# Epilogue of a graph layer: where the table additions, the biases and the output bias are computed

## What is computed

```python
h = relu(layernorm(x))                                     # nodes, 6250 x 64
msg = relu(concat(h[dst], edge_attr) @ W1a + b1a) @ W1b + b1b
summed = segment_sum(msg, src); counts = segment_sum(1, src)
agg = summed / max(counts, 1)
out = x + relu(concat(h, agg) @ W2a + b2a) @ W2b + b2b
```

## Time and profile before

| what | us |
|---|---|
| median of three runs | 1584.05 |
| profiled execution | 1595.53 |
| its span | 1593.7 |
| TensorE busy | 1468.8 (92%) |
| VectorE busy | 1422.9 (89%) |
| Pool busy | 1215.1 (76%) |
| ScalarE busy | 1023.7 (64%) |

### The profile page before, as it was taken

One profiled execution on the slowest core, in us unless ns is written; L12 is line 12 of the kernel. 1 busy time (PEld: TensorE's weight loads), 2 busy tenths in 40 slices (PEclk: granted clock), 3 DMA queues, 4 the chain that ended last, 5 costly groups with the idle time before them and its releaser, 6 DMA issues. The chain is left out here.

```text
span 1593.7 us, 76970 instructions
## 1 busy us (share of the span) xinstructions
PE 1468.8 (92%) x31106; PEld 1401.0 (88%) x31106; DVE 1422.9 (89%) x4766; ACT 1023.7 (64%) x2192; POOL 1215.1 (76%) x804
## 2 busy tenths in 40 slices
PE   4378999999999989999999999999999999999937
PEld 3167999999999989999999999999999999999935
DVE  7977999999999979899999989999999999999937
ACT  5167666666666656667676766766766666666405
POOL 5347878778787778878787787788777788777864
PEclk8679999999999999999999999999999999999978
DMA  5657766776767666676676766766766677676643
GB/s 173 232 111 117 124 109 111 124 110 110 125 109 125 107 99 110 110 123 113 110 125 110 120 110 112 121 109 117 117 111 120 106 117 118 109 121 108 96 60 122
DMA packets 278693, 186.57 MB, mean 117 GB/s; under 512 B 190215, under 2 KB 274692, under 8 KB 277569
## 3 DMA queue, kind: packets, MB, share of 16 engines
q1 hardware_dynamic: 173358, 152.31, 38.8%
q0 software_dynamic: 104976, 29.30, 26.8%
HBM read 147.32 MB, written 34.17 MB: 114 GB/s over the span
## 5 line engine op out<-in xcount | busy, mean ns | idle before, releaser
L523 POOL DMA_INDIRECT sums<-vv,sidx x726 | 1158.5, 1596 | 328.8 <-issue 172.4
L1242 PE MATMUL l_ps<-area 128*128 128x64 bf16 (+1 forms) x21000 | 766.7, 193 | 7.7 <-issue 1.6
L1242 PEld LDWEIGHTS l_ps<-area 128*128 128x128 bf16 x21000 | 730.8, 98 | 28.7 <-issue 14.5
L698 ACT ACTIVATE area<-l_ps 64x392 bf16<-64x392 f32 x1400 | 684.5, 489 | 74.1 <-PE l_ps L1228 49.0
L949 DVE TENSOR_SCALAR area<-iota,local 128x640 bf16<-128x640 int16 x1400 | 482.8, 409 | 4.9
L1228 PE MATMUL l_ps<-r_d,oh 128*128 128x196 bf16 x4200 | 482.6, 249 | 2.8 <-ACT area L698 1.4
L1228 PEld LDWEIGHTS l_ps<-r_d,oh 128*128 128x128 bf16 x4200 | 345.2, 97 | 17.0 <-ACT area L698 3.2
L934 DVE TENSOR_SCALAR oh<-iota,rank 128x640 bf16<-128x640 int16 x846 | 285.1, 403 | 0.0
L681 ACT ACTIVATE r_d<-z_ps 128x384 f32<-128x384 f32 x423 | 207.6, 491 | 84.6 <-PE z_ps L1198 74.2
L686 ACT ACTIVATE vv<-c_ps 128x396 f32<-128x396 f32 x121 | 60.5, 500 | 265.3 <-PE c_ps L1217 179.3
L956 DVE TENSOR_TENSOR dense<-l_ps,dense 128x325 f32<-128x325 f32 x280 | 136.5, 488 | 83.8 <-PE l_ps L1242 83.2
(11 more groups left out here) (131 smaller groups left out, 736.9 us busy)
## 6 DMA issues: line engine op xcount, KB each, us to landing
ids_s<-ids SPq DMA_DIRECT2D x246, 192.0 KB
et_d<-in_e_t SPq DMA_DIRECT2D x143, 192.0 KB
ids_d<-ids SPq DMA_DIRECT2D x143, 192.0 KB
et_s<-in_e_t SPq DMA_DIRECT2D x123, 192.0 KB
sums<-vv,sidx POOLq DMA_INDIRECT x726
sums<-dense POOLq DMA_DIRECT2D x3, 1657.5 KB
wp_d<-p_table SPq DMA_DIRECT2D x286, 15.8 KB
wp_s<-p_table SPq DMA_DIRECT2D x246, 15.8 KB
```

The source lines that it names most:

```text
L523: nc.gpsimd.indirect_dma_start(out=sums[t][:, :], out_offset=bass.IndirectOffsetOnAxis(ap=index, axis=0), in_=rows, in_offset=None, comput ...
L698: ins = nc.scalar.activation(routed[on, t.div(MACRO).mod(2), first:second + 1:second - first, t.mod(MACRO), :], bank[on, :, :], ACT.Copy)
L1242: ins = nc.tensor.matmul(l2_ps[h][:, u * W:u * W + w], oh2[:, g, u * P:(u + 1) * P], rows[:, PARTS[r]:PARTS[r] + w], start=g % MACRO == 0 ...
```

## The change

Ahead of the loop, Pool no longer adds b2b to `xs`. VectorE does it behind the loop, after three small memsets. In the epilogue, Pool's two additions of a turn are tab 0 += dense and tab 1 += tab 2, without a wait between them, and VectorE adds tab 1 to tab 0 (add_tables). The sign of the count is taken on 4 columns instead of 256, its transpose has 2 rows a pair, and ScalarE copies these two rows (met_keep). TensorE adds a third product to the hidden bank: `bias_rows` (two rows, q for each tile of a pair) by the two rows of signs. b2a goes into the relu as ScalarE's bias, and the relu reads the PSUM bank; base and hidden_sum are gone. The weights get one more column, and q is computed as two rows and copied by one small ScalarE operation. Leads and orders of the stages change on VectorE, ScalarE and TensorE. The lines of declarations and of semaphores' names are left out here.

```diff
...
-C_B2A = C_B1B + 1
+C_B2A = C_B1B + 2
...
-        wcq = sb("wcq", [P, P + 1])
+        wcq = sb("wcq", [P, P])
+        bias_rows = sb("bias_rows", [2, P])
...
-        met = sb("met", [P, 2, NPG, D], bf16)
+        met = sb("met", [P, 2, NPG], bf16)
...
-        base_st = stage[:, 0:2 * HALF].rearrange("p (b c) -> p b c", b=2)
+        met_st = stage[0:2, 0:2 * HALF].rearrange("p (b c) -> p b c", b=2)
...
-                pool.wait_ge(rowb_in, 16)
-                pool.wait_ge(xc_ready, done(NTURNS))
-                b2b = rowb[:, 1:2, :].to_broadcast([P, NTP, D])
-                nc.gpsimd.tensor_tensor(xs[:], xs[:], b2b, ALU.add).then_inc(xb_ready, 1)
...
-                pool.sem_inc(pool_part, START)
...
-                    for k in range(1, TABLES):
-                        if k > 1:
-                            pool.wait_ge(pool_part, done(m * (TABLES - 2) + k - 1))
-                        nc.gpsimd.tensor_tensor(tab[0][:, part], tab[0][:, part], tab[k][:, part],
-                                                ALU.add).then_inc(pool_sum if k == TABLES - 1 else pool_part, 1)
+                    for total, more in ((tab[0], dense), (tab[1], tab[2])):
+                        nc.gpsimd.tensor_tensor(total[:, part], total[:, part], more[:, part], ALU.add).then_inc(pool_sum, 1)
...
             def _(act):
...
-                          hid_ready, base_ready):
+                          hid_ready, met_kept):
...
-                nc.scalar.activation(wcq[:], c_ps[0][:, 0:P + 1], ACT.Copy).then_inc(wc_ready, 1)
+                nc.scalar.activation(wcq[:], c_ps[0][:, 0:P], ACT.Copy).then_inc(wc_ready, 1)
+                nc.scalar.activation(bias_rows[:], c_ps[0][0:2, P:2 * P], ACT.Copy).then_inc(wc_ready, 1)
...
                     def split(kind, g, r):
...
                 def hidden(b, m):
-                    act.wait_ge(hsum_ready, done(m + 1))
-                    nc.scalar.activation(hid_st[:, b, :], hid_st[:, b, :], ACT.Relu).then_inc(hid_ready, 1)
+                    act.wait_ge(hid_raw, done(m + 1))
+                    act.wait_ge(res_raw, done(m - 1))
+                    nc.scalar.activation(hid_st[:, b, :], z_ps[b][:, 0:HALF], ACT.Relu, bias=wts[:, C_B2A:C_B2A + 1]).then_inc(hid_ready, 1)
...
                 def met_rows(b, m):
...
-                    count = total[:, bass.ds(m * NPG, NPG), D:W].to_broadcast([P, NPG, D])
-                    nc.scalar.activation(met[:, b, :, :], count, ACT.Sign).then_inc(met_ready, 1)
...
-                def base(b, m):
...
+                    nc.scalar.activation(met[:, b, :], total[:, bass.ds(m * NPG, NPG), D], ACT.Sign).then_inc(met_ready, 1)
...
+                def met_keep(b, m):
...
-                    act.wait_ge(hsum_ready, done(m - 1))
-                    nc.scalar.activation(base_st[:, b, :], met_ps[b][:, 0:HALF], ACT.Identity, bias=wts[:, C_B2A:C_B2A + 1],
-                                         scale=wcq[:, P:P + 1]).then_inc(base_ready, 1)
...
-                pipelined([(2, mean_t_keep), (1, base), (1, hidden), (3, met_rows)])
+                    act.wait_ge(hid_raw, done(m - 1))
+                    nc.scalar.activation(met_st[:, b, :], met_ps[b][0:2, 0:HALF], ACT.Copy).then_inc(met_kept, 1)
...
+                pipelined([(1, hidden), (2, mean_t_keep), (2, met_keep), (3, met_rows)])
...
             def _(dve):
...
-                def add_dense(b, m):
+                def add_tables(b, m):
...
-                    dve.wait_ge(pool_sum, done(m + 1))
-                    nc.vector.tensor_tensor(tab[0][:, part], tab[0][:, part], dense[:, part], ALU.add).then_inc(added, 1)
+                    dve.wait_ge(pool_sum, done(2 * m + 2))
+                    nc.vector.tensor_tensor(tab[0][:, part], tab[0][:, part], tab[1][:, part], ALU.add).then_inc(added, 1)
...
-                def hidden_sum(b, m):
-                    dve.wait_ge(hid_raw, done(m + 1))
-                    dve.wait_ge(base_ready, done(m + 1))
-                    dve.wait_ge(res_raw, done(m - 1))
-                    nc.vector.tensor_tensor(hid_st[:, b, :], z_ps[b][:, 0:HALF], base_st[:, b, :], ALU.add).then_inc(hsum_ready, 1)
...
-                dve.wait_ge(xb_ready, 1)
...
+                b2b = rowb[:, 1:2, :].to_broadcast([P, NTP, D])
+                nc.vector.tensor_tensor(xs[:], xs[:], b2b, ALU.add).then_inc(xb_ready, 1)
...
-                pipelined([(3, add_dense), (3, counts), (3, inverse), (1, hidden_sum), (3, mean_of), (0, result)])
+                dve.wait_ge(xb_ready, 1)
...
+                pipelined([(4, add_tables), (3, inverse), (0, result), (4, counts), (3, mean_of)])
...
             def _(pe):
...
-                nc.tensor.matmul(c_ps[0][:, P:P + 1], wts[:, C_W2A_BOT:C_W2A_BOT + P], wts[:, C_B1B:C_B1B + 1],
+                nc.tensor.matmul(c_ps[0][0:2, P:2 * P], wts[:, C_B1B:C_B1B + 2], wts[:, C_W2A_BOT:C_W2A_BOT + P],
...
-                pe.wait_ge(wc_ready, 1)
+                pe.wait_ge(wc_ready, 2)
...
                 def hidden(b, m):
...
-                    pe.wait_ge(hsum_ready, done(m - 1))
+                    pe.wait_ge(met_kept, done(m + 1))
+                    pe.wait_ge(hid_ready, done(m - 1))
                     nc.tensor.matmul(z_ps[b][:, 0:HALF], wts[:, C_W2A_TOP:C_W2A_TOP + P], ht[:, bass.ds(m * HALF, HALF)],
...
-                    nc.tensor.matmul(z_ps[b][:, 0:HALF], wcq[:, 0:P], at_st[:, b, :], start=False, stop=True).then_inc(hid_raw, 1)
+                    nc.tensor.matmul(z_ps[b][:, 0:HALF], bias_rows[:], met_st[:, b, :], start=False, stop=False)
+                    nc.tensor.matmul(z_ps[b][:, 0:HALF], wcq[:], at_st[:, b, :], start=False, stop=True).then_inc(hid_raw, 1)
...
                 def met_t(b, m):
...
-                    pe.wait_ge(base_ready, done(m - 1))
+                    pe.wait_ge(met_kept, done(m - 1))
...
-                        t = nc.tensor.matmul(met_ps[b][:, j * P:(j + 1) * P], pair(met, b, j), ident_b[:], start=True, stop=True)
+                        t = nc.tensor.matmul(met_ps[b][0:2, j * P:(j + 1) * P], met[:, b, 2 * j:2 * j + 2], ident_b[:],
+                                             start=True, stop=True)
...
                 def out_rows(b, m):
...
-                pipelined([(1, hidden), (2, mean_t), (0, out_rows), (2, met_t)])
+                pipelined([(1, hidden), (2, mean_t), (2, met_t), (0, out_rows)])
...
 def kernel(x, src, dst, edge_attr_64, L0_gnn_u, L0_gnn_W1a, L0_gnn_b1a, L0_gnn_W1b, L0_gnn_b1b, L0_gnn_W2a, L0_gnn_b2a,
...
-             np.tile(b1b, 2)[:, None], np.tile(b2a, 2)[:, None]]
+             twice(b1b[:, None]), np.tile(b2a, 2)[:, None]]
...
```

More of the change, by code:

```diff
@@ L311, in gnn_kernel @@
             "dsum_ready dpick_ready dsidx_ready dense_ended sums_done")
-        tables_in, pool_part, pool_sum, added, xb_ready, pads_ready = sems("tables_in pool_part pool_sum added xb_ready pads_ready")
+        tables_in, pool_sum, added, xb_ready, pads_ready = sems("tables_in pool_sum added xb_ready pads_ready")
         counts_ready, inverse_ready, a_ready, at_raw, at_ready = sems("counts_ready inverse_ready a_ready at_raw at_ready")
-        met_ready, met_raw, base_ready = sems("met_ready met_raw base_ready")
-        hid_raw, hsum_ready, hid_ready, res_raw, res_ready = sems("hid_raw hsum_ready hid_ready res_raw res_ready")
+        met_ready, met_raw, met_kept = sems("met_ready met_raw met_kept")
+        hid_raw, hid_ready, res_raw, res_ready = sems("hid_raw hid_ready res_raw res_ready")
         READS = (1, 3)
@@ L769, in _ @@
                           *zsum_ready, *gidx_ready, slots_ready, local_ready, nodes_ready, summed, dsum_ready, dpick_ready, dsidx_ready,
-                          added, counts_ready, inverse_ready, a_ready, hsum_ready, res_ready):
+                          added, counts_ready, inverse_ready, a_ready, res_ready):
                     dve.sem_inc(s, START)
```

## The result

The changed kernel is slower. Six executions of it have a median of 1594.62 us (1591.52 to 1600.79), six of the kernel before 1584.46 us; the ratio is 1.007, with a 95% interval from 1.0044 to 1.0095, so some 7 to 15 us. I had forecast 1582.2 us. The traced execution took 1600.79 us with a span of 1598.8 (before 1595.53 and 1593.7).

| stretch, us | before | after | difference | forecast |
|---|---|---|---|---|
| first scatter issued | 95.75 | 87.68 | -8.1 | -7.5 |
| the scatter issue beside VectorE's long addition | 1.55 | 5.04 | +3.5 | 0 |
| first table addition (Pool's) to the last result's end | 41.1 | 58.9 | +17.9 | +5.7 |

A forecast was written before the change was run, and what follows sets the result against it. Bounds: VectorE's chain ahead of the loop; in the epilogue TensorE at 1.2 GHz, then a 2.28 us cycle across engines. -7.5 ahead and +5.7 in the epilogue gave -1.8 us: 1584.05 to 1582.2, range 1577.5 to 1587.5.

The forecast's parts named there:

- Pool's addition ahead of the loop: Ahead of the edge loop: without Pool's addition, VectorE's scaling takes 1.66 us instead of 9.18, saving 7.5 us.
- Rival B: Ahead of the loop: the freed time is not passed on, under 2.5 of 7.5 us arriving; 1589.8 us, chance 0.10.
- VectorE's addition costs nothing: Behind the loop: the output-bias addition, at most 5.4 us, fits VectorE's 19.52 us wait before the epilogue.
- rival C: Behind the loop: VectorE's long addition holds up Pool's last scatters for all its 5.4 us; 1587.7 us, chance 0.06.
- The third product: Epilogue, TensorE: the added two-row product takes 0.43 us at 2.4 GHz and 0.86 at 1.2 GHz.
- the ring: Epilogue: the cycle of waits between TensorE and ScalarE sets a turn, growing from 2.28 to 2.65 us.
- The ten turns: Epilogue at 2.4 GHz: ten turns of 2.65 us bring the hidden products from number 2 to number 12, at 1593.4.
- The clock: Epilogue: TensorE's clock rises from 1.2 to 2.4 GHz where it did before, at about 1564.7 us.
- rival D: Epilogue: TensorE's clock rises two turns later, 2 x 1.5 = +3.0 us; 1585.3 us, chance 0.12.
- Mean 0 queued behind add 1: Epilogue start: the first mean waits one table addition longer on VectorE, some 4 us; first transpose at 1558.24.
- A: Epilogue: the two-row product is cheap, a turn stays near 2.3 us, epilogue +1.2; 1577.8 us, chance 0.22.

The follow-up runs named there:

- e3: Kernel before with only the output-bias addition moved from Pool ahead of the loop to VectorE behind it; ratio 0.9968.
- e9_late_add: Kernel before with the output bias added by VectorE behind the loop, but only once Pool's last scatter has landed; ratio 0.9967.
- e1_pad128: Changed kernel with the bias product over 128 rows, 126 of them zeros, instead of 2; ratio 1.0006.
- e7: Kernel before with one superfluous f32 product of 2 rows by 256 columns added per epilogue turn; ratio 1.0018.
- e2: Changed kernel with the bias product left out, so its result lacks q for nodes with an edge; ratio 0.9966.
- e10: Changed kernel with the bias product over 128 rows and VectorE's output-bias addition only after Pool's last scatter has landed; ratio 0.9999.
- k64: Changed kernel with the zero-padded bias product over 64 rows instead of 2; one run, 1610.82 us.

## Why the prediction was wrong

*Pool's addition ahead of the loop: right.* I had 7.5 us, the trace has 8.1; by runs, e3 and e9_late_add gain 0.3%, 5 us, with intervals from 1 to 9. That all 8.1 arrive is neither shown nor excluded. Rival B, under 2.5 us arriving, isn't excluded by these intervals either; the middle value speaks against it.

*VectorE's addition costs nothing: wrong in the trace.* It holds a scatter by 1.7 to 3.7 us of issue in eight kernels, for an addition that runs 3.56 rather than at most 5.4. I gave rival C 0.06 on the ground that scatters take 1.596 in a loop in which VectorE is busy. But that mean is over VectorE's short instructions of the loop, many of them with one input; it says nothing on a single long one with two SBUF inputs. The row that bore on this stood in the earlier trace rows, Pool holding VectorE up for the length of one long addition, and the Trainium skill's rule cited in the prediction named this form. The price is small against the rest, and late or early addition can't be told apart in time.

*The third product, the step that failed.* "If the columns set its time, it is L1302's: 0.86 at 1.2 GHz, 0.43 at 2.4", and "from above 0.54". Measured it is 0.62, it makes the product ahead of it 0.06 and the one behind it 0.11 longer, and at 1.2 GHz it is 1.15. Every f32 product in the rows I went by had 128 rows of weights. e1_pad128 shows that with 128 rows the forecast of the ring was right (2.66 for 2.65), e7 shows the price in the kernel before, e2 that nothing else of the epilogue costs. The ten turns that I had at 2.4 GHz, each 0.40 longer, are 4.0 us.

*The clock, sized by the wrong kernel.* I let it rise where it had, and rival D allowed two turns more, 3.0 us. It rose after 34 us (48 in the repeat) instead of 14. From the first L1290 to the thirteenth I had 33.75 us and the trace has 46.5; 4.0 of the difference is the product's length in those ten turns, so 8.7 is the longer turns at 1.2 GHz (5.04 for 4.15) and their number (five for about one and a half). That the two-row product is what does it in this epilogue is shown by e1, e10 and e2: padded to 128 rows or left out, the rise comes after 12, 17 and 14 us. k64 and e7 (17) can't be told from these, so a two-row product in each turn isn't enough by itself: in the order of the kernel before it leaves the clock nearly where it was. What in the new epilogue goes with it, and how the chip comes to it, isn't shown.

*The start.* Mean 0 queued behind add 1 was right: the first transpose stands 7.34 us behind the first table addition, where the forecast had 8.28 (1558.24 - 1549.96). The 0.9 less is VectorE's second addition waiting until 5.09 instead of 5.53 us, and 2.25 from there to the transpose instead of 2.75.

With the stretch at +17.9 instead of +5.7 (-0.9 start, +4.0, +8.7, +0.4 at the end), and the scatter's +3.5, the sum by the traces is +13.3 instead of -1.8. Of my rivals C happened beside the forecast, D happened at several times its size, and A (a cheap two-row product), which had the largest chance, lay on the wrong side: I had bounded the unseen operation below by "near nothing" and above by its neighbour, and it cost more than the neighbour.

## What to carry to other kernels

Replacing a ScalarE or VectorE operation by a matmul of two rows is not a small matmul: in a TensorE-bound turn it cost more than the same product over 128 zero-padded rows, and in this epilogue, though not in that of the kernel before, it kept the clock at 1.2 GHz for several turns more, which was the larger part. Bound an operation that no row shows above its nearest neighbour too, and try it padded. Before moving a long VectorE operation with two SBUF inputs, see what Pool does at its new place; the time it frees at the old one was the only gain of this change, and e3's single edit has it without the rest.

## What was unexpected of the hardware

- A f32 product over 256 columns at 2.4 GHz: 0.62 us with 2 rows, 0.63 with 64, 0.44 to 0.53 with 128, and 0.06 to 0.11 more for the product on either side. The Trainium skill (TensorE: Matmul & The Clock Gate, Back-to-back issue gap) gives the spacing by formulas in the number of columns, with no term for the rows; by them the bias product would cost what its neighbours do. The measurement decides.
- With the two-row product in each turn of the changed epilogue TensorE stayed at 1.2 GHz through 20 us of unbroken work; in the epilogue before, with such a product, it was at 2.4 GHz after 17 us. A clock of 2.4 GHz brought into the epilogue fell 3 to 10 us after the first table addition, with or without that product.
- A scatter issue of 1.55 us stood still for a VectorE addition of 3.56 us: 5.04 and 5.21 where they started together. In eight traces the held scatter ended 1.41 to 1.44 us after the addition, while one that had run 0.31 us when the addition began still took only 1.57.
